# The clamp of the squared norms moved from VectorE into the final multiplication of the rotated rows, with another order table

## What is computed

```python
def l2norm(t):
    return t / jnp.clip(jnp.linalg.norm(t, axis=-1, keepdims=True), 1e-12)
...
def _layer(x, wqkv, qs, ksc, wo, lg, lb, w1, b1, w2, b2):
    h = shift_token(x)
    q, k, v = jnp.split(h @ wqkv, 3, axis=-1)          # 8 heads of 64 each
    q = l2norm(q) * qs
    k = l2norm(k) * ksc
    q, k = rotary_xpos(q, k)                           # t*cos*scale + rotate_half(t)*sin*scale
    x = x + local_attention(q, k, v) @ wo
    ...                                                # layer norm of the shifted x, then w1, gelu gate, w2
    return x
```

## Time and profile before

| | us |
|---|---|
| three runs | 1961.76, 1965.38, 1968.51 |
| median | 1965.38 |
| the profiled execution | 1963.38 |
| its span, first to last instruction | 1961.3 |
| busy: PE, ACT, DVE, POOL | 1836.3, 1377.8, 1244.0, 903.6 |
| chunks of the layers phase, as 16 stretches | 77.4, then 78.8 to 81.0, last two 77.5 and 70.6 |

### The profile page before, as it was taken

One profiled execution on the slowest core, in us unless ns is written; L12 is line 12 of the kernel. 1 busy time (PEld: TensorE's weight loads), 2 busy tenths in 40 slices (PEclk: granted clock), 3 DMA queues, 4 the chain that ended last, 5 costly groups with the idle time before them and its releaser, 6 DMA issues.

```text
span 1961.3 us, 47714 instructions
## 1 busy us (share of the span) xinstructions
PE 1836.3 (94%) x17808; PEld 1565.5 (80%) x17808; DVE 1244.0 (63%) x4126; ACT 1377.8 (70%) x3998; POOL 903.6 (46%) x1302
## 2 busy tenths in 40 slices
PE   6999999999999789999999999999999999999998
PEld 4788788788778568788788887887888878888787
DVE  4544543454443467777777777777777776777765
ACT  5886987878688465766857757668577585675854
POOL 3533543434344553735626437255364562654621
PEclk9999999999999889999999999999999999999989
DMA  4321320422324511110110101305112112010110
GB/s 146 100 76 55 116 87 34 116 76 77 87 75 150 180 47 28 39 53 23 47 45 23 54 17 50 122 15 168 37 39 63 34 47 66 18 60 25 42 47 28
DMA packets 125018, 128.11 MB, mean 65 GB/s; under 512 B 26632, under 2 KB 100082, under 8 KB 124788
## 3 DMA queue, kind: packets, MB, share of 16 engines
q1 hardware_dynamic: 121620, 118.77, 19.5%
q10 hardware_dynamic: 3168, 6.29, 0.9%
HBM read 72.44 MB, written 36.85 MB: 56 GB/s over the span
## 4 chain that ended last, share of the span: by engine, by line
PE 58%; ACT 11%; DVE 11%; POOL 11%; issue 5%; DMA 2%; SPq 1%; DVEq 0%; POOLq 0%; ACTq 0%
PE a_bank L630 15%; PE f_bank L1555 10%; PE f_bank L1416 9%; PE f_scores L1570 5%; POOL f_prob L1380 5%; PE a_o_bank L727 4%; ACT f_prob L1639 3%; PE f_o_bank L1530 3%; PE f_scores L1497 3%; PE a_bank L712 2%; PE a_scores L704 2%; POOL f_qk_tok L1368 2%; DVE f_scores L1713 2%; POOL f_norm L1362 1%; POOL a_prob L610 1%
## 5 line engine op out<-in xcount | busy, mean ns | idle before, releaser
L610 POOL TENSOR_SCALAR a_prob<-a_prob,a_row_inv,a_gate 128x128 f32<-128x128 f32 x512 | 226.3, 459 | 379.9 <-DVE a_row_inv L948 379.9
L1380 POOL TENSOR_SCALAR f_prob<-f_prob,f_row_inv 128x192 f32<-128x192 f32 x512 | 244.6, 495 | 319.6 <-DVE f_row_inv L1721 319.6
L1416 PE MATMUL f_bank<-weights,f_actT 128*128 128x512 f32 x1152 | 300.7, 406 | 1.5 <-DVE f_actT L1672 1.5
L1555 PE MATMUL f_bank<-f_hT,f_w 128*128 128x256 f32 x2112 | 269.1, 283 | 1.0 <-DVE f_gu L1775 1.0
L1555 PEld LDWEIGHTS f_bank<-f_hT,f_w 128*128 128x128 f32 x2112 | 258.4, 188 | 4.0 <-DVE f_gu L1775 2.7
L1416 PEld LDWEIGHTS f_bank<-weights,f_actT 128*128 128x128 f32 x1152 | 209.6, 191 | 48.2 <-ACT f_probT L1587 3.1
L1368 POOL TENSOR_TENSOR f_qk_tok<-f_qk_tok,tables 128x512 f32<-128x512 f32 x128 | 164.8, 1308 | 149.3 <-DVE f_sin_part L1689 149.3
L1639 ACT ACTIVATE f_prob<-f_scores,f_neg_max 128x192 f32<-128x192 f32 x512 | 207.9, 426 | 17.2 <-DVE f_neg_max L1713 15.9
L1713 DVE CUSTOM_DVE_ANT_0 f_scores<-f_scores,f_mask 128x192 f32<-128x192 f32 x512 | 166.3, 387 | 69.3 <-PE f_scores L1497 69.2
L1362 POOL TENSOR_TENSOR f_norm<-f_norm,f_minus_half 128x16 f32<-128x16 f32 x64 | 189.3, 2959 | 34.4 <-DVE f_norm L1681 31.5
L630 PE MATMUL a_bank<-a_xT,weights 128*128 128x512 f32 x768 | 195.6, 405 | 1.5 <-DVE a_wgate L917 1.5
(11 more groups left out here) (143 smaller groups left out, 4021.6 us busy)
## 6 DMA issues: line engine op xcount, KB each, us to landing
split_weights<-a_hi_lo SPq DMA_DIRECT2D x16, 512.0 KB, 3.0
x_next<-states SPq DMA_DIRECT2D x32, 256.0 KB, 3.2
tables<-scaled_tables SPq DMA_DIRECT2D x16, 512.0 KB, 6.0
f_x<-states SPq DMA_DIRECT2D x16, 512.0 KB, 5.3
split_weights<-a_hi_lo SPq DMA_DIRECT2D x12, 682.0 KB, 4.6
weights<-split_weights ACTq DMA_DIRECT2D x6, 1024.0 KB, 9.3
f_w<-split_weights SPq DMA_DIRECT2D x4, 1280.0 KB, 11.7
f_v_crossed<-f_v SPq DMA_DIRECT2D x40, 128.0 KB, 2.4
```

Of the source, the lines that this page charges most:

```text
L610: last = nc.gpsimd.tensor_scalar(part, part, row_inv[:, a % 2, head, t:t + 1], gate[:, half, t, h:h + 1], ALU.mult, ALU.mult)
L1380: last = nc.gpsimd.tensor_scalar(part, part, row_inv[:, a % 2, head, t:t + 1], 1.0, ALU.mult, ALU.mult)
L1416: last = nc.tensor.matmul(out, lhs(c, a), rhs(c, b), start=(i == 0), stop=(i == len(order) - 1))
L1555: mm = nc.tensor.matmul(out[:, which * PART:(which + 1) * PART], w1[:, wp, c, col:col + P], hT[:, hp, c, columns_of(a // FH)], start=(i == ...
```

## The change

Three things change. VectorE's clamp (line 1681) and its semaphore `clamped` go; GpSimd's power waits for the second sum of squares itself. The clamp's purpose is met behind the power instead: the last instruction of `rope_sum` becomes one with two operations, which takes the smaller of the inverse norm and 1e12 and multiplies the row by it. Its operands are exchanged: the broadcast inverse norm comes first, the row second. And `ORDER` is another permutation of the same 109 steps.

```diff
--- before.py
+++ after.py
@@ -990,20 +990,20 @@
              "add_attended": 1, "load_wqkv": 1, "load_others": 1, "cross_values": 1, "up": 12, "down": 12, "out": 2}
 F_PREPARE = ("load_wqkv", "load_tables", "transpose_x", "project_qk", "rope", "rope_sum", "transpose_qk", "project_v", "cross_values")
 F_FIRST_HALF = ("shift_keys", "load_wqkv", "load_others")
-ORDER = [("softmax", 0), ("softmax", 1), ("scores", 0), ("scores", 1), ("weigh", 0), ("scores", 2), ("weigh", 1), ("transpose_x", 0),
-         ("transpose", 0), ("softmax", 2), ("transpose", 1), ("scores", 3), ("weigh", 2), ("project_qk", 0), ("load_x", 0), ("take_o", 0),
-         ("softmax", 3), ("values", 0), ("values", 1), ("load_x1", 0), ("weigh", 3), ("rope", 0), ("scores", 4), ("transpose", 2),
-         ("project_qk", 1), ("softmax", 4), ("scores", 5), ("weigh", 4), ("rope_sum", 0), ("values", 2), ("transpose", 3),
-         ("project_qk", 2), ("softmax", 5), ("scores", 6), ("values", 3), ("weigh", 5), ("rope", 1), ("transpose_qk", 0), ("take_o", 1),
-         ("transpose", 4), ("scores", 7), ("softmax", 6), ("weigh", 6), ("project_qk", 3), ("project_o", 0), ("rope_sum", 1), ("weigh", 7),
-         ("transpose", 5), ("softmax", 7), ("load_tables", 0), ("load_others", 0), ("shift_keys", 0), ("shift_front", 0), ("shift_back", 0),
-         ("take_o", 2), ("values", 4), ("values", 5), ("transpose", 6), ("project_v", 0), ("transpose_qk", 1), ("transpose", 7),
-         ("ln_stats", 0), ("ln_apply", 0), ("take_o", 3), ("rope", 2), ("values", 6), ("values", 7), ("project_v", 2), ("transpose_h", 0),
-         ("project_o", 1), ("rope_sum", 2), ("up", 0), ("up", 1), ("up", 2), ("project_v", 1), ("ln_stats", 1), ("ln_apply", 1),
-         ("down", 0), ("down", 1), ("project_v", 3), ("up", 3), ("down", 2), ("transpose_h", 1), ("cross_values", 0), ("rope", 3),
-         ("load_wqkv", 0), ("up", 4), ("down", 3), ("up", 5), ("up", 6), ("up", 7), ("down", 4), ("up", 8), ("up", 9), ("rope_sum", 3),
-         ("down", 5), ("down", 6), ("transpose_qk", 2), ("up", 10), ("up", 11), ("down", 7), ("down", 8),
-         ("add_attended", 0), ("transpose_qk", 3), ("down", 9), ("out", 0), ("out", 1), ("down", 10), ("down", 11)]
+ORDER = [("softmax", 0), ("scores", 0), ("scores", 1), ("weigh", 0), ("weigh", 1), ("softmax", 1), ("transpose_x", 0), ("scores", 2),
+         ("transpose", 0), ("softmax", 2), ("transpose", 1), ("scores", 3), ("weigh", 2), ("project_qk", 0), ("softmax", 3), ("values", 0),
+         ("take_o", 0), ("load_x1", 0), ("weigh", 3), ("rope", 0), ("values", 1), ("scores", 4), ("transpose", 2), ("project_qk", 1),
+         ("softmax", 4), ("scores", 5), ("transpose", 3), ("weigh", 4), ("rope_sum", 0), ("project_qk", 2), ("values", 2), ("scores", 6),
+         ("softmax", 5), ("weigh", 5), ("rope", 1), ("take_o", 1), ("values", 3), ("transpose_qk", 0), ("transpose", 4), ("scores", 7),
+         ("softmax", 6), ("weigh", 6), ("project_qk", 3), ("project_o", 0), ("transpose", 5), ("softmax", 7), ("values", 4), ("values", 5),
+         ("rope_sum", 1), ("load_tables", 0), ("load_others", 0), ("weigh", 7), ("take_o", 2), ("ln_stats", 0), ("transpose", 6),
+         ("project_v", 0), ("transpose_qk", 1), ("transpose", 7), ("ln_apply", 0), ("take_o", 3), ("rope", 2), ("values", 6), ("values", 7),
+         ("project_v", 2), ("transpose_h", 0), ("project_o", 1), ("rope_sum", 2), ("shift_keys", 0), ("shift_front", 0), ("up", 0),
+         ("up", 1), ("ln_stats", 1), ("up", 2), ("project_v", 1), ("down", 0), ("down", 1), ("project_v", 3), ("ln_apply", 1), ("up", 3),
+         ("down", 2), ("transpose_h", 1), ("rope", 3), ("up", 4), ("down", 3), ("up", 5), ("up", 6), ("up", 7), ("down", 4),
+         ("shift_back", 0), ("up", 8), ("down", 5), ("up", 9), ("rope_sum", 3), ("load_x", 0), ("cross_values", 0), ("transpose_qk", 2),
+         ("down", 6), ("up", 10), ("up", 11), ("down", 7), ("down", 8), ("down", 9), ("transpose_qk", 3), ("add_attended", 0), ("out", 0),
+         ("out", 1), ("load_wqkv", 0), ("down", 10), ("down", 11)]
 
 
 def layers_phase(nc, kept, attended_end, states, attended, out, wqkv_in, wo_in, w1_in, w2_in, bias_in, rows_in, tables_in, masks):
@@ -1125,7 +1125,6 @@
         v_crossing = count("v_crossing", {"cross_values": 1}, unit=64)
         keys_shifted = count("keys_shifted", {"shift_keys": 1}, unit=16)
         raw_taken = count("raw_taken", {"project_qk": 2})
-        clamped = count("clamped", {"project_qk": 1})
         norm_ready = count("norm_ready", {"project_qk": 1})
         sin_ready = count("sin_ready", {"rope": 1})
         cos_ready = count("cos_ready", {"rope": 1})
@@ -1357,7 +1356,7 @@
 
             def norms(it, a):
 
-                pool.wait_ge(clamped.sem, clamped.past(it, ("project_qk", a)))
+                pool.wait_ge(emptied.sem, emptied.past(it, ("project_qk", a), KEY))
                 n = norm[:, a % TILES].rearrange("p i h -> p (i h)")
                 nc.gpsimd.tensor_tensor(n, n, minus_half[:], ALU.pow).then_inc(norm_ready.sem, 1)
 
@@ -1677,9 +1676,6 @@
                     nc.vector.tensor_reduce(norm[:, a % TILES, which, :], square[:, which, :].rearrange("p (h d) -> p h d", d=DH), AXIS.X,
                                             ALU.add).then_inc(emptied.sem, 1)
 
-                dve.wait_ge(emptied.sem, emptied.past(it, ("project_qk", a), KEY))
-                nc.vector.tensor_scalar(norm[:, a % TILES], norm[:, a % TILES], 1e-24, None, ALU.max).then_inc(clamped.sem, 1)
-
             def rope(it, a):
 
                 if a % TILES == 0:
@@ -1696,8 +1692,8 @@
                 nc.vector.tensor_tensor(place, place, sin_part[:], ALU.add).then_inc(rope_added.sem, 1)
                 dve.wait_ge(norm_ready.sem, norm_ready.past(it, ("project_qk", a)))
                 dve.wait_ge(rope_added.sem, rope_added.past(it, ("rope_sum", a)))
-                nc.vector.tensor_tensor(by_head(place), by_head(place), norm[:, a % TILES].unsqueeze(3).broadcast_to([P, 2, F_HEADS, DH]),
-                                        ALU.mult).then_inc(roped.sem, 1)
+                nc.vector.scalar_tensor_tensor(out=by_head(place), in0=norm[:, a % TILES].unsqueeze(3).broadcast_to([P, 2, F_HEADS, DH]), scalar=1e12,
+                                               in1=by_head(place), op0=ALU.min, op1=ALU.mult).then_inc(roped.sem, 1)
 
             for it, kind, a in program:
                 layer = layer_of(it)
```

## The result

The changed kernel takes **1933.3 us** (median of four executions, 1928.08 to 1938.84) against 1964.41 (1961.76 to 1968.51) for the kernel before on the same chip: ratio 0.984, interval 0.9807 to 0.9874. The forecast was 1944 with a range of its own from 1938 to 1949, the whole range 1931 to 1963. The profiled execution took 1934.84, its span is 1932.7, 28.6 us less than before. In the new code the lines behind the order table have moved: up to `project_qk` by one (the first is L1415 for L1416), the addition is L1692, the fused multiplication L1695.

What follows compares the result with a forecast made beforehand. TensorE's waits, with GpSimd as second critical chain, were taken to bound the kernel. Thirteen chunks at 1.6 us (20.8), plus 1.6, less 1, gave 21.4 us saved: 1944 us, own range 1938 to 1949, whole range 1931 to 1963.

Steps and rivals of the forecast that it cites:

- The bound: In the layers phase, TensorE's waits count, not busy shares; GpSimd is the second critical chain in mid-chunk.
- The clamp: Without VectorE's clamp, GpSimd's power starts 0.2 us earlier; its weighings gain 0.65 us and most of 2.0 us.
- The multiplication: VectorE's fused minimum and multiplication costs 0 to +0.17 us each over the plain 1.23 us; taken as 0.
- (a): TensorE does transpose_x ahead of scores 2, filling half of a 1.95 us gap: gain 0.8 us a chunk.
- (b): values 2 goes behind transpose 3 and project_qk 2: a new bank wait of 0.45 to 0.5 us, taken as -0.5.
- (c): ScalarE takes softmax 3 ahead of the first values pair's copy: cover for unit 3's weighing, nothing for TensorE.
- (f): ScalarE fetches the second layer's projection weights at a chunk's end, landing 9.3 us after issue: costs 1 us once.
- The sum: Over the chunks: 1.6 us in each of thirteen, 0.8 for two others, less 1 for the weights: 21.4 us.
- rival 4: Both stretched weighings vanish and the bank wait stays under 0.1 us: 2.2 us a chunk, 1934 us; chance 0.08.
- Rival 1: GpSimd stays the bound, stretched elsewhere; transpose 7 comes only 0.8 + 0.2 us earlier: 1953 us; chance 0.15.
- Rival 3: VectorE's fused multiplication runs at a third of the rate, 3.3 us for 1024 elements: 1978 us; chance 0.10.
- Rival 2: TensorE's waits return as bank waits behind project_qk and at the next transposes: 1963 to 1965 us; chance 0.12.

Runs made afterwards that it cites:

- e1: The clamp edit with the old order table, against the kernel before: 1935.8 us, ratio 0.986.
- e2: The new order table with the clamp kept on VectorE, against the kernel before: 1931.8 us, ratio 0.984.
- e7: The changed kernel with the plain multiplication, the bound on the inverse norm left out: 1934.8 us, ratio 0.986 to the kernel before.
- e5: The kernel before, clamp kept, with only transpose_x moved ahead of scores 2: 1950.7 us, ratio 0.994.
- e4: The changed kernel with values 2 back in its old place ahead of transpose 3: 1931.7 us, ratio 0.986 to the kernel before.
- e9: The kernel before, clamp kept, with transpose_x ahead of scores 2 and softmax 3 ahead of take_o 0: 1935.3 us, ratio 0.987.
- e10: The kernel before, clamp kept, with transpose_x ahead of scores 2 and values 2 behind project_qk 2: 1951.0 us, ratio 0.995.
- e11: The changed kernel with transpose_x's transposes done twice, a repeat of e3: 1923.2 us, ratio 0.981 to the kernel before.
- a1: The changed kernel run again, on the chip of e9, e10 and e11: 1932.9 us, ratio 0.986 to the kernel before.
- e3: The changed kernel with transpose_x's transposes done twice to fill TensorE's gap: 1925.8 us, ratio 0.983 to the kernel before.
- e6: The changed kernel with a spare clamp on VectorE that nobody waits for: 1935.9 us, ratio 0.987 to the kernel before.
- a0: The changed kernel run again, on the chip of e1, e2 and e5: 1932.1 us, ratio 0.984 to the kernel before.

## Why the prediction was right, and where not

**The number.** 1933.3 us lies in the range as a whole, but below the forecast's own (1938 to 1949), and the sign that I gave for it was missed on the same side: a chunk of 77.0 us and not 77.4 to 77.8. The mechanism was right for the most part, the size was not.

**The bound.** Right: TensorE's waits and GpSimd as a second chain, not the shares of busy time.

**The clamp.** The mechanism was right and undersized. GpSimd idles 1.42 us in front of the first power rather than 1.61: the 0.2 us that I took. The weighings of units 4 and 6 are at 1.64 us, as said. But I let the clamp edit carry only a part of the sum and wrote that transpose 7 needed the gains of both; e1 gets 28 us without the table, e2 31 without the edit. The step that failed is that of adding up per part. What costs is the stretched weighing of unit 6, and it is free of stretching in e1 and in e2 alike (1.6 us): either part puts that weighing clear of VectorE's addition, and the waits at transpose 7 can be saved only once.

**The multiplication.** Right: 1226 against 1231 ns, and e7 agrees.

**The table.** (a) Right: from the start of `scores` 0 to that of `scores` 3 it was 8.72 us and is 7.99 (in the undisturbed chunk 939.52 less 931.57, 7.95): 0.73 to 0.77 against 0.8, and e5, which has this alone, gives 12 to 14 us, some 0.8 in each chunk. With the stretched weighing gone it is worth less: the undisturbed chunks of e1, which lack it, take 77.4 and 76.7 us in turn, those of the changed kernel 77.0 and 76.1 or 76.2. (b) The wait was named rightly and is 0.27 us, not 0.45 to 0.5; e4 shows that the move has no net price. (c) Wrong: this move is the one that matters when the clamp stays (e9 against e10, 16 us). With the clamp gone it matters little. (f) The weights land 10.1 us after issue (median) instead of 9.3; the chunk that waits for them took 77.2 us where its peers took 77.0: 0.2, not 1 (0.6 in e11, nothing in a1, e3, e4 and e7).

**The sum.** The 14 chunks between the first and the last gave 24.0 us in the two profiles, although 7 of them are slowed by the clock; six of the other seven gave 1.9 to 2.7 each, not 1.6, and the seventh, which had no stall before, 0.8. e11, without the falls in these chunks, is 38.0 us below the kernel before on its chip. The last chunk gave 2.6 (66.5 to 63.9), of it a wait for the layer norm that went from 1.79 to 0.98 us, and some from the clock (0.92 to 0.95); I had 0.8 for two chunks together. About 1.1 us lies ahead of all chunks: the first matmuls of `layers_phase` start at 657.75 and not 658.89, behind code that the change doesn't touch, and the first chunk gave 0.8. So the forecast lay 11 us too high as the net of two terms of opposite sign: the gain of a chunk was put too small (2.2 us, rival 4's number, is the better one), and the clock took back about 10 us of what was won (1932.9 against 1923.2), which no step spoke of. That the miss is not larger is luck: without the falls it would have been some 20 us.

**The rivals.** Rival 1 fell, since the weighings of units 4 and 6 are at 1.64 us. Rival 3 fell with 1226 ns. Rival 2 fell on its forecast of the time, but one sentence of it holds under the new table: VectorE's own time is worth next to nothing (e6). Rival 4 named 1934 and came nearest. Of its two conditions one held, both stretched weighings are gone; the other did not, the bank wait is 0.27 us and not under 0.1; and its number leaves out the 10 us of the clock, so that it was met so closely is luck too.

The rule of the Trainium skill that I weighed ("SBUF — State Buffer", "Who interferes with whom") did better for the power than I had allowed. For the clamp I had read too much into it: the sentence is about an instruction with two SBUF inputs, and the clamp has one, so its 1.32 us neither agree with that sentence nor contradict it. The timelines of the changed kernel, VectorE and GpSimd:

```profile
1029.68 1.23 DVE L1692 TENSOR_TENSOR f_qk_tok<-f_qk_tok,f_sin_part 128x1024 f32<-128x1024 f32 x1 [0.21 <-POOL f_qk_tok L1367]
...
1042.55 1.29 DVE L1692 TENSOR_TENSOR f_qk_tok<-f_qk_tok,f_sin_part 128x1024 f32<-128x1024 f32 x1
```

```profile
1029.58 2.93 POOL L1361 TENSOR_TENSOR f_norm<-f_norm,f_minus_half 128x16 f32<-128x16 f32 x1
...
1042.68 3.93 POOL L1361 TENSOR_TENSOR f_norm<-f_norm,f_minus_half 128x16 f32<-128x16 f32 x1
```

When the power starts first, both run undisturbed; when the addition starts 0.13 us first, the power takes 1.0 us more. That the power needs what they share only at its start would explain both, but it is an inference. It costs nothing that can be seen here: 13 chunks of e9 have such a power, the shortest of all (75.64 us) among them.

## What to carry to other kernels

When an instruction on one engine is held by another engine's, look at the phase of the two before pricing the edit by the instruction's time: here 0.17 us of work that came less than 0.1 us too late was held for over 1 us, and two unrelated edits (28 and 31 us alone, 31 together) each undid what followed from it, so their gains don't add. Cost such a stall through to the end of the chain it delays: the same stall was free in e2 and e6 and cost 1 to 2 us a chunk where it made the chain meet a second instruction. Try the parts alone before crediting either. When a tuned kernel loses its other waits, a gap of 1 us on TensorE can begin to cost through the clock; here work without use in it paid (9.7 us).

## What the hardware did that I had not expected

- A gap of 0.93 us at a chunk's start is followed in 7, 9 and 6 of 14 chunks (the result, a0, a1; only 2 in e7) by a fall of the granted clock to 1.2 GHz 2.1 to 4.2 us later, for 1.5 or 2.6 us lost. Filling it with eight more transposes (0.9 us) ends nearly all of the falls (1 of 14 in e3, none in e11). Why some chunks have a fall and others not stays open.
- A clamp of 0.2 us on VectorE that starts 0.066 us or more ahead of GpSimd's second two-input instruction passes (32 of 32 in six traces); one that starts 0.061 us or less ahead of it is held until it has ended (64 of 64).
- GpSimd's power over 16 elements takes 2.91 us, or 3.9 when VectorE's addition of two SBUF inputs has started just before it (0.13 to 0.19 us in the changed kernel).
